# Second halves of adj blocks issued by GpSimd's queue instead of SyncE's, in a six-pass graph network kernel

## What is computed

```python
x = layernorm(x + relu((adj @ x) @ kernel + bias))
u, v = x, v_node_feats
for _ in range(3):
    v = mlp(adj @ u, uv_W1, uv_b1, uv_W2, uv_b2, uv_W3, uv_b3)
    u = mlp(adj @ v, vu_W1, vu_b1, vu_W2, vu_b2, vu_W3, vu_b3)
x = layernorm(x + v)
```

## Time and profile before

| | |
|---|---|
| median of 3 runs | 1171.18 us (1171.15 to 1171.29) |
| the profiled execution | 1171.81 us |
| its span, from the first to the last instruction | 1170.0 us |
| granted TensorE clock | 0.999 |
| TensorE busy | 1154.7 us, 99% |
| VectorE busy | 737.4 us, 63% |
| ScalarE busy | 661.1 us, 57% |
| DMA | 261.6 MB, 224 GB/s on average |

### The profile page before, as it was taken

One profiled execution on the slowest core, in us unless ns is written; L12 is line 12 of the kernel. 1 busy time (PEld: TensorE's weight loads), 2 busy tenths in 40 slices (PEclk: granted clock), 3 DMA queues, 4 the chain that ended last, 5 costly groups with the idle time before them and its releaser, 6 DMA issues.

```text
span 1170.0 us, 13668 instructions
## 1 busy us (share of the span) xinstructions
PE 1154.7 (99%) x5224; PEld 950.8 (81%) x5224; DVE 737.4 (63%) x889; ACT 661.1 (57%) x809; POOL 0.2 (0%) x4
## 2 busy tenths in 40 slices
PE   7999999999999999999999999999999999999997
PEld 5788888888888888888888888888888888887775
DVE  7897676458555555555545746554566555658886
ACT  7765554346554555555444754554566454557885
POOL 0000000000000000000000000000000000000000
PEclk9999999999999999999999999999999999999999
DMA  9988785568356646555656736655665565569891
GB/s 383 401 294 324 254 268 190 207 216 287 122 205 213 214 158 210 203 188 180 215 181 216 258 110 220 212 171 182 205 226 187 191 205 209 195 223 357 290 322 53
DMA packets 72209, 261.60 MB, mean 224 GB/s; under 512 B 8016, under 2 KB 8656, under 8 KB 71120
## 3 DMA queue, kind: packets, MB, share of 16 engines
q1 hardware_dynamic: 72000, 260.61, 64.1%
q10 hardware_dynamic: 144, 0.13, 0.0%
HBM read 258.61 MB, written 2.10 MB: 223 GB/s over the span
## 4 chain that ended last, share of the span: by engine, by line
PE 92%; DMA 3%; DVE 2%; ACT 2%; issue 1%; SPq 0%; DVEq 0%; ACTq 0%
PE agg_ps L833 28%; PE agg_ps L826 28%; PE agg_ps L819 28%; PE pre_ps L752 4%; DMA adj_raw<-in_adj 3%; PE hid_ps L713 1%; PE hid_ps L715 1%; PE hid_ps L714 1%; DVE adj_lo L705 1%; ACT adj_hi L590 1%; PE hid_ps L774 1%; PE hid_ps L788 0%; ACT hid L484 0%; DVE stats L603 0%; ACT resid L505 0%
## 5 line engine op out<-in xcount | busy, mean ns | idle before, releaser
L705 DVE TENSOR_TENSOR adj_lo<-adj_raw,adj_hi 128x1024 fp32r<-128x1024 f32 x488 | 576.5, 1221 | 230.8 <-ACT adj_hi L590 224.8
L819 PE MATMUL agg_ps<-adj_hi,feat_hi 128*128 128x512 f32 x1536 | 609.1, 397 | 7.5 <-ACT adj_hi L590 7.4
L826 PE MATMUL agg_ps<-adj_hi,feat_lo 128*128 128x512 f32 x1536 | 599.2, 390 | 0.0
L590 ACT ACTIVATE adj_hi<-adj_raw 128x1024 fp32r<-128x1024 f32 x488 | 492.8, 1052 | 95.1 <-PE agg_ps L833 80.2
L833 PE MATMUL agg_ps<-adj_lo,feat_hi 128*128 128x512 f32 x1536 | 475.1, 391 | 0.3 <-DVE adj_lo L705 0.2
L819 PEld LDWEIGHTS agg_ps<-adj_hi,feat_hi 128*128 128x128 f32 x1536 | 289.0, 188 | 69.9 <-issue 10.7
L826 PEld LDWEIGHTS agg_ps<-adj_hi,feat_lo 128*128 128x128 f32 x1536 | 289.0, 188 | 62.3 <-issue 3.4
L833 PEld LDWEIGHTS agg_ps<-adj_lo,feat_hi 128*128 128x128 f32 x1536 | 287.9, 188 | 63.3 <-DVE adj_lo L705 3.2
L484 ACT ACTIVATE hid<-hid_ps,params 128x512 f32<-128x512 f32 (+1 forms) x80 | 54.5, 681 | 57.5 <-PE hid_ps L715 50.6
L555 ACT ACTIVATE in_hi<-part 128x512 fp32r<-128x512 f32 x24 | 15.2, 634 | 110.4 <-DVE part L694 110.4
L484 ACT ACTIVATE post<-pre 128x512 f32<-128x512 f32 x39 | 24.6, 630 | 79.8 <-DVE pre L674 79.8
(11 more groups left out here) (63 smaller groups left out, 251.3 us busy)
## 6 DMA issues: line engine op xcount, KB each, us to landing
adj_raw<-in_adj SPq DMA_DIRECT2D x472, 512.0 KB, 5.6
adj_raw<-in_adj SPq DMA_DIRECT2D x8, 1024.0 KB, 8.1
resid<-in_x SPq DMA_DIRECT2D x8, 256.0 KB, 8.1
out<-resid SPq DMA_DIRECT2D x7, 256.0 KB, 7.3
params<-in_weights SPq DMA_DIRECT2D x1, 386.0 KB, 5.0
b_row<-in_bias_rows SPq DMA_DIRECT2D x1, 128.0 KB, 5.5
out<-resid ACTq DMA_DIRECT2D x1, 128.0 KB, 2.0
out<-resid SPq DMA_DIRECT2D x1, 128.0 KB, 2.1
```

Source lines behind the costliest of these rows:

```text
L590: act.activation(adj_hi[:, plan.slot[b], i * CHUNK:(i + pieces) * CHUNK], adj_raw[:, h % RAW, 0:pieces * CHUNK], ACT.Copy).then_inc(adj_hi ...
L705: dve.tensor_tensor(adj_lo[:, plan.slot[b], slot], adj_raw[:, h % RAW, 0:pieces * CHUNK], adj_hi[:, plan.slot[b], slot].bitcast(F32), ALU. ...
L819: pe.matmul(group_bank(g), feat_hi[feats][:, tile(src, i)], adj_hi[:, plan.slot[b], piece(i)], start=start, stop=False)
L826: pe.matmul(group_bank(g), feat_lo[feats][:, tile(src, i)], adj_hi[:, plan.slot[b], piece(i)], start=False, stop=False)
```

## The change

SyncE skips the second halves from the ninth block on (b >= 8 and i = 2). GpSimd gets a program that goes through the same list, skips the blocks below 8 and the first halves, waits for the same count of adj_lo_ready, and issues the same transfer into the same slot with the same semaphore.

```diff
@@ block.sync
                 if h == LOAD_PARAMS:
                     sp.dma_start(params[:, P:], weights[:, P:]).then_inc(params_loaded, 16)
                     sp.dma_start(b_row[:, P:], bias_rows[P:].partition_broadcast(P)).then_inc(params_loaded, 16)
+                if b >= WHOLE and i:
+                    continue
                 if h >= RAW:
                     sp.wait_ge(adj_lo_ready, h - RAW + (2 if b < WHOLE and i == 0 else 1))
@@ behind block.sync
+        @block.gpsimd
+        def _(pool):
+            for h, (b, i, pieces) in enumerate(plan.loads):
+                if b < WHOLE or i == 0:
+                    continue
+                pool.wait_ge(adj_lo_ready, h - RAW + 1)
+                row, col = plan.blocks[b]
+                pool.dma_start(adj_raw[:, h % RAW, 0:pieces * CHUNK], adj[row, col][:, i * CHUNK:(i + pieces) * CHUNK])\
+                    .then_inc(adj_loaded[h % RAW], 16)
```

## The result

The changed kernel takes 1172.99 us (median of 16 runs, 1172.27 to 1173.78) against 1171.26 us for the kernel before (16 runs, 1171.03 to 1171.46). The ratio is 1.0016, 95% interval 1.0009 to 1.0022: 1.1 to 2.6 us slower, 1.7 by the medians. That is smaller than the 0.2% named in the prediction and inside its range, but it is a real loss and larger than the +1.0 us forecast. The runs also scatter over 1.5 us, where those of the kernel before scatter over 0.4. One execution of the kernel before, in the series that stands beside experiments 1 to 3 and the first kernel of experiment 8, took 5011.79 us and is left out of every ratio.

What follows compares the result with a forecast made beforehand. TensorE was taken to bound the kernel, with late adj transfers mattering only before 60 us. 0.65 + 0.65 - 0.3 gave +1.0 us, so 1172.2 us for the median (1172.8 profiled); range 1170.2 to 1176.3 us.

Steps and rivals of the forecast that it cites:

- The stage: Cost arises between 20 and 60 us; after 60 us, 5.6 us of cover on TensorE, priced at 0.
- SyncE's side: 236 issues of 0.328 us leave SyncE, 77 us, worth nought because its issuing does not bound the chain.
- Latency inside the line: GpSimd's transfers, 20 to 60 us: up to 4.8 us of extra issue latency costs nothing, being time in line.
- The order of landing: 20 to 60 us: two queues share full engines, so landing order costs; three parts sum to +1.0 us.
- Term 1: SyncE's queue before 60 us: x at half the rate delays first halves, +0.65 us, +0.97 at most with weights and bias.
- Term 2: Phase of a block's two halves running side by side, 20 to 60 us: +0.65 us, bounds 0 and +1.3.
- Term 3: TensorE before 60 us: its small lead covers some of the delay, -0.3 us.
- A: GpSimd's issue slow per transfer: at 4 us about 1207 us, 4 in 100; slow first one 1177 us, 6 in 100.
- B: GpSimd and VectorE hinder each other, subtractions 5 to 10% longer, 20 to 60 us: 1174 to 1176 us, 8 in 100.
- C: Fixed cost at start or end for GpSimd's own queue, 0 to 4 us, around 1175 us, 5 in 100.
- D: Two queues fill the DMA engines better before 60 us: -1.0 us, 1170.2 us, 12 in 100.
- E: Nothing changes; TensorE's lead covers the order or streams fall half a period apart: 1171.2 us, 24 in 100.

Runs made afterwards that it cites:

- experiment 1: Against the kernel before, GpSimd issues second halves only from h = 64 on, SyncE everything else: 1171.47 us, ratio 1.0001.
- experiment 2: Against the kernel before, GpSimd issues only the second halves of h = 17 to 45, SyncE all others: 1173.31 us, ratio 1.0017.
- experiment 3: Against the kernel before, GpSimd issues the first halves from the ninth block on, SyncE the second ones: 1173.58 us, ratio 1.0018.
- experiment 8: Three variants of the change: x and weights on GpSimd too, 1172.66 us; the same with x held back, 1172.31; weights at h = 30 on SyncE, 1172.38.
- experiment 9: Against the kernel before, GpSimd issues both halves from the ninth block on, their x and all weights: 1172.55 us, ratio 1.0013.
- experiment 5: Against the kernel before, GpSimd issues second halves from h = 25 on, SyncE everything before: 1175.04 us, ratio 1.0033.
- experiment 7: Against the changed kernel, GpSimd waits for two subtractions more before each issue up to h = 45: 1174.73 us, 1.0031 of the kernel before.
- experiment 6: Against the kernel before, h = 17 alone goes through GpSimd, all others through SyncE: 1171.19 us, ratio 1.0000.

## Why the prediction was right, and which term was too small

**The stage.** Right. All of it arises in the stage before 60 us (experiments 1 and 2), and TensorE never gets it back. The cover after 60 us was enough for GpSimd's transfers; the price of 0 holds, even with twice as many of them (experiment 9). Two of the signs that the prediction named came out otherwise: TensorE waited 1.3 us for adj_hi where 0.5 had been, and the rate of the stretch was 395 GB/s, outside its 400 to 420. In experiments 5 and 7, which lose 3.8 and 3.5 us, the rate is 391 and 384, in the three kernels of experiment 8, which lose 1.0 to 1.4, it is 407 to 408. I read the fall as a consequence of late halves (slots become free later, transfers start later); no run tests that.

**SyncE's side.** Right: 236 issues fewer there and nothing gained.

**Latency inside the line.** "Extra latency of up to 4.8 us costs nothing by itself" was wrong in general. 3.4 us of delay at the issue came out as 1.9 us at the landing (experiment 7). It did no harm in the change because GpSimd is hardly later than SyncE: 0.53 against 0.33 us per issue, and the quickest landing of a half after 60 us is 3.4 against 3.1 us.

```profile
L490 POOL DMA_DIRECT2D adj_raw<-in_adj x192: 527/527/544, 63.1 to 1026.4; - x192
...
DMA to landing us min/median/max: 3.4/5.4/9.2
```

**The order of landing.** The mechanism was right, the terms were not. Term 1 (x and weights at half the rate, 0.65, at most 0.97) had a core in the weights, by the medians 0.6 us (experiment 8); what x costs these runs don't separate. It also left out the x that stands ahead of h = 16. Term 2, the phase, was taken as 0.65 with 1.3 us as its upper bound; that is the mis-sized one. It reckoned with two streams already side by side. In truth the new queue is empty when the old one holds a line of halves and x, and what is put into it goes past that line: all of h = 17 and most of h = 19 (by the packets 1.84 halves) moved before h = 16 landed, which came 2.0 us late; in experiment 2 h = 18 came 3.5 us late, and in experiment 5 h = 24 at least 2.58. One half is no bound. Term 3, 0.3 us of cover, was wrong in both directions: at h = 16 the landing was 2.02 us late and TensorE's adj_lo product only 1.08, at h = 24, which set the cost in this trace, 1.96 us late became 1.95 and nothing was covered. So terms 1 and 2 together, 1.3 us, stood against 1.96. Put together, 0.65 + 0.65 - 0.3 gave +1.0; measured were +1.7 by the medians and +1.9 in the traces.

**Rivals.** A is wrong: 0.53 us per transfer, not 2.6, and the first one, 0.66 us, is no exception worth the name. B is wrong: the subtraction takes 30.80 us / 27 = 1.141 us between 20 and 60 us, 1.137 before. GpSimd isn't hindered either: of its 236 issues 162 ran for more than half of their time beside a subtraction of VectorE, and but for the first one (664 ns) all took 527 to 544 ns. None ran beside the scaling of L618 (L630 in the changed kernel), so what that would do is not shown. C is wrong: 1.8 us around the span in both, and experiment 1 shows no fixed cost. D is wrong: the rate of the stretch was 395 instead of 404 GB/s, so lower. E is refuted by the interval.

By the Trainium skill, page "SBUF — State Buffer", section "Who interferes with whom", a subtraction of two tensors should not keep GpSimd from writing descriptors, which the Trainium skill itself calls inferred; the trace agrees, with 527 to 544 ns. The Trainium skill, page "DMA: Bandwidth & Descriptors", has, in "Queues, rings and completion order", that each DMA engine takes turns between the queues for which it has work. The runs agree: two halves went past one that took 12.52 us to land.

**Open.** Why the changed kernel scatters over 1.5 us was not tried. Others with two active queues before 60 us scattered over 0.5 (h = 17 alone) to 3.2 us (GpSimd waits longer), the kernel before over 0.4 to 1.1 us. The traces of the changed kernel and of experiment 2 show that the order of landing differs between executions, but only one trace of each kernel was read. How much of the 1.7 us belongs to the weights, and what x costs, is not settled either.

## What to carry to other kernels

A second DMA queue added no bandwidth here, where the DMA engines were full (395 against 404 GB/s), but it changes who comes first: what enters an empty queue goes past what waits in the other one. If a consumer takes the transfers in a fixed order, keep them in one queue while it has no lead, and switch only where the line is short or the lead covers it, here from h = 64 on. To price it, estimate how many transfers the other queue will move before the last one of the line lands, times the time of one; a bound of one transfer is too low (1.84 halves and 2.0 us at h = 16), and counting all that is issued meanwhile is too high (three halves there). Small transfers that go into the empty queue count too, as x does in experiments 8 and 9.

## What the runs showed of the hardware

- A transfer of 512 KB made by GpSimd costs 0.53 us of GpSimd's time and about 0.3 us more to landing than one made by SyncE (3.4 against 3.1 us at the least). From h = 17 to h = 23, a line made by GpSimd alone landed within 0.12 us of one made by SyncE, at 403 GB/s.
- A transfer in a full line of SyncE came 1.39 us later for one half issued on GpSimd's queue (experiment 6), and 2.58 us later than in the trace of before where GpSimd's queue had moved 2.6 halves (experiment 5); in one line on the full engines a half takes 1.28 us.
- With two active queues the same transfer landed at 44.12 us in one execution and at 42.95 in another (h = 24, the change and experiment 2); with one queue at 42.16 and 41.61 (before and experiment 1).
- 162 of GpSimd's 236 issues ran mostly beside a subtraction of two tensors on VectorE and took no longer than the others, 527 to 544 ns.
- ScalarE's queue beside SyncE's did the same as GpSimd's: 6.9 against 9.5 us to landing.
- Two transfers of 64 KB, one of them a broadcast of 512 bytes to each partition, ahead of h = 24 in SyncE's line were worth 1.86 us of its landing against the trace of the changed kernel and 0.69 us against that of experiment 2; their bytes alone (131072) would make 0.3 us at 404 GB/s, or 0.65 at half of it.
